# Query and key biases folded into the projection weights, and the feed-forward transposes moved to another accumulator bank with a new order of work

## The reference, cut to what matters

```
n  = (x - mean) * rsqrt(var + eps)            # over the 128 features
q  = (n * qn_w  + qn_b)  @ q_w + q_b          # 16 heads of 8
kv = (n * kvn_w + kvn_b) @ kv_w + kv_b        # k, v
q, k = rotary(q, x), rotary(k, x)             # cos/sin per token, scaled by a radius
q, k = layernorm over the 8 of a head
a  = softmax(q k^T / sqrt(8)) v @ out_w + out_b
x1 = x + a
z  = layernorm(x1); zp = z shifted one token back
r  = sigmoid((mu_r*z + (1-mu_r)*zp) @ W_r^T)
k2 = relu((mu_k*z + (1-mu_k)*zp) @ W_k^T) ** 2
x2 = x1 + r * (k2 @ W_v^T)
```

## Time and profile before

| | |
|---|---|
| runs, median | 1365.89 us |
| profiled execution | 1367.37 us, its span 1365.6 us |
| PE busy | 1284.8 us (94%) |
| DVE busy | 1122.7 us (82%) |
| ACT busy | 901.9 us (66%) |
| POOL busy | 504.9 us (37%) |
| steps of A with all stages (c = 6 to 31) | 26, mostly of 18.11 us |
| first and last row maximum (L790) | 35.5 and 605.1 us |

### The profile page before, as it was taken

How to read it: one execution, slowest core, us unless ns; L and a number is a source line. 1 busy time by engine, 2 the same in 40 slices (tenths; PEclk the granted TensorE clock), 3 DMA queues, 4 the chain that set the end, 5 groups by cost and what they waited for, 6 DMA issues and landing times.

```text
span 1365.6 us, 32982 instructions
## 1 busy us (share of the span) xinstructions
PE 1284.8 (94%) x10579; PEld 852.4 (62%) x10579; DVE 1122.7 (82%) x2849; ACT 901.9 (66%) x2504; POOL 504.9 (37%) x815
## 2 busy tenths in 40 slices
PE   7889999999999999888999999999999998999996
PEld 5445555555555555545566666666666665888885
DVE  5888999999999999876888888888888875778786
ACT  3278888888888888876565566556655653555563
POOL 5446666666666666533111111111111100232322
PEclk9999999999999999999999999999999999999998
DMA  2222332223333323210100010000000001232220
GB/s 80 77 76 81 82 79 76 73 78 80 82 91 103 99 69 84 67 51 17 32 28 29 28 49 28 30 28 28 27 30 25 20 17 41 79 87 82 85 86 27
DMA packets 101963, 79.61 MB, mean 58 GB/s; under 512 B 13780, under 2 KB 95124, under 8 KB 101796
## 3 DMA queue, kind: packets, MB, share of 16 engines
q1 hardware_dynamic: 100820, 76.99, 20.0%
q10 hardware_dynamic: 976, 0.54, 0.2%
HBM read 49.70 MB, written 27.79 MB: 57 GB/s over the span
## 4 chain that ended last, share of the span: by engine, by line
PE 49%; issue 1%; DVE 1%; ACT 1%; POOL 0%; POOLq 0%; DVEq 0%; ACTq 0%
PE b_psZ L1410 4%; PE b_psD L1331 4%; PE b_psZ L1342 4%; PE b_g L1394 4%; PE d_psO L1954 4%; PE b_g L1381 4%; PE d_psH L1946 4%; PE b_psM L1443 2%; PE b_psR L1387 2%; PE b_psL L1372 2%; PE b_psR L1403 2%; PE b_psD L1433 2%; PE b_psM L1455 1%; PE d_psG L1972 1%; PE d_psV L1985 1%
## 5 line engine op out<-in xcount | busy, mean ns | idle before, releaser
L790 DVE TENSOR_REDUCE a_MX<-a_psS 128x4 f32<-128x1024 f32 x248 | 303.2, 1223 | 44.6 <-PE a_psS L304 41.2
L591 ACT ACTIVATE a_PT<-a_psE 128x512 f32<-128x512 f32 x504 | 275.1, 604 | 59.3 <-PE a_psE L321 56.4
L1811 POOL TENSOR_TENSOR b_SWB<-b_b2col,b_SW 128x128 f32<-128x128 f32 x65 | 38.8, 597 | 346.2 <-ACT b_SW L1526 346.2
L335 PE MATMUL a_psV<-a_PT,a_VX 128*32 128x256 f32 x2048 | 137.0, 385 | 0.2 <-ACT a_PT L591 0.2
L1545 ACT ACTIVATE b_TH<-b_psZ 128x512 f32<-128x512 f32 x65 | 38.9, 598 | 128.7 <-PE b_psZ L1342 124.3
L304 PE MATMUL a_psS<-a_KS,a_QS 48*128 48x256 f16 x992 | 97.7, 275 | 22.1 <-DVE a_MX L790 20.6
L321 PE MATMUL a_psE<-a_QS,a_KS 50*128 50x256 bf16 x1008 | 97.5, 270 | 3.1 <-ACT a_PT L591 3.1
L1565 ACT ACTIVATE b_PR<-b_psL,b_mx 128x128 f32<-128x128 f32 x260 | 93.1, 369 | 0.9
L304 PEld LDWEIGHTS a_psS<-a_KS,a_QS 48*128 48x128 bf16 x992 | 29.1, 94 | 103.1 <-issue 48.2
L335 PEld LDWEIGHTS a_psV<-a_PT,a_VX 128*32 128x32 f32 x2048 | 53.4, 109 | 50.5 <-issue 27.5
L1693 DVE SCALAR_TENSOR_TENSOR b_HH<-b_TH,b_psZ 128x512 f32<-128x512 f32 x65 | 44.8, 689 | 44.1 <-ACT b_TH L1545 44.0
(11 more groups left out here) (298 smaller groups left out, 3426.4 us busy)
## 6 DMA issues: line engine op xcount, KB each, us to landing
a_KS<-kparts SPq DMA_DIRECT2D x63, 192.0 KB
a_QS<-qparts SPq DMA_DIRECT2D x126, 96.0 KB
qparts<-a_QP SPq DMA_DIRECT2D x64, 96.0 KB, 2.2
a_X<-x_in SPq DMA_DIRECT2D x32, 128.0 KB, 2.3
kparts<-a_KP SPq DMA_DIRECT2D x64, 64.0 KB, 2.1
x<-a_X SPq DMA_DIRECT2D x32, 128.0 KB, 1.8
b_X<-x SPq DMA_DIRECT2D x32, 128.0 KB, 2.2
zT<-b_XT SPq DMA_DIRECT2D x32, 128.0 KB, 1.7
```

The source lines that it names most:

```text
L335: mm = nc.tensor.matmul(psV[32 * h:32 * h + 32, 0:T], VX[:, b % UV, kt, at:at + 32], PT[:, gg, kt, h, :], start=(gg == 0 and kt == 0), sto ...
L591: nc.scalar.activation(PT[:, g % 2, :, h + s, :], shifted_bank(b, p, s), ACT.Exp).then_inc(S["exp"], 1)
L790: nc.vector.reduce_max(MX[:, b % 2, :].rearrange("q (s n) -> q s n", s=2)[:, :, 2 * p:2 * p + 2], score_banks(b, p)[:], AX.X).then_inc(S[" ...
```

## The change

The layer norm's output sums to zero over its 128 features, so the last feature is minus the sum of the others. The changed kernel leaves it out and puts a constant 1.0 in its place: `Z` gets only 127 normalised columns and a last column of ones, written once. The weights are rebuilt in the opening: each row minus the last row, times the gain, and as last row the bias. For this, PE has a new function `fold_weights` (five products of 128 columns and one of one column), DVE makes `gains`, and ACT copies the result to `wall`. Two constants are loaded more (`last`, 128x128, and `brow`, one row). With the biases in the weights, `cosine` and `sine` are one instruction of 512 columns each.

The second half moves work: `fz_t` writes bank psA for sequences before 26, ACT makes all four copies in slot 3, `ot` moves from slot 4 to 5; on PE, `on_t` and `z_t` move from slot 5 to slot 4, `ffn_kr` is split, with its k product placed between the scores and the shifted scores of slot 5 and its r products after, and `out_proj` goes before `hr_t`; on DVE, `x1` goes before `normed`.

```diff
-        nc.scalar.activation(wall[:, 0:P], wraw[:, 0:P], ACT.Copy, scale=vecs[:, 0:1]).then_inc(S["wall"], 1)
...
+        def weights():
+            act.wait_ge(S["param_ps"], 2)
+            nc.scalar.activation(wall[:, 0:2 * P], psS[:, 0, 0, :], ACT.Copy).then_inc(S["wall"], 1)
...
+        def fold_weights():
+            pe.wait_ge(const_in, EARLY)
+            for j in range(2):
+                pe.wait_ge(S["coefs"], 2 * j + 3)
+                nc.tensor.matmul(psS[:, 0, 0, j * P:(j + 1) * P], brow[:, 2, :], brow[:, j, :], start=True, stop=False)
+                nc.tensor.matmul(psS[:, 0, 0, j * P:(j + 1) * P], gains[:, j, :], wraw[:, j * P:(j + 1) * P], start=False, stop=True).then_inc(S["param_ps"], 1)
+            pe.wait_ge(S["coefs"], 6)
+            nc.tensor.matmul(psS[:, 1, 0, 0:P], gains[:, 2, :], wraw[:, 2 * P:3 * P], start=True, stop=True)
+            nc.tensor.matmul(psS[:, 1, 0, P:P + 1], last[:], wraw[:, 3 * P:3 * P + 1], start=True, stop=True).then_inc(S["param_ps"], 1)
...
         def cosine(b):
-            for k in range(2):
-                nc.vector.scalar_tensor_tensor(out=YC[:, k * T:(k + 1) * T], in0=psA[:, k * T:(k + 1) * T], scalar=bcol[:, k:k + 1], in1=cosT[:],
-                                               op0=ALU.add, op1=ALU.mult).then_inc(S["cosed"], 1)
+            nc.vector.tensor_tensor(YC[:].rearrange("q (k t) -> q k t", k=2), psA[:].rearrange("q (k t) -> q k t", k=2),
+                                    cosT[:].unsqueeze(1).broadcast_to([P, 2, T]), ALU.mult).then_inc(S["cosed"], 1)
...
         def fz_t(b):
+            if b < B - 6:
+                wait(pe, "square", b + 6)
+                wait(pe, "centred", b + 6)
...
+                to = (psE[0][:, 0, :] if b == B - 2 else psC if b >= B - 6 else psA)[:, t * P:(t + 1) * P]
...
-        def ffn_kr(b):
+        def ffn_k(b):
             wait(pe, "square", b + 6)
             wait(pe, "centred", b + 6)
+            wait(pe, "fzT", b, per=4)
             wait(pe, "mixed", b, per=2, done=1)
             nc.tensor.matmul(psA[:, 0:T], wk_t[:], FX[:, 1, :], start=True, stop=True)
+
+        def ffn_r(b):
             wait(pe, "mixed", b, per=2)
```

More of the change, by code:

```diff
@@ L87, in phase_a @@
     wraw, wall = sb("wraw", [P, 3 * P + 1]), sb("wall", [P, 3 * P + 1])
+    last, gains, brow = sb("last", [P, P]), sb("gains", [P, 3, P]), sb("brow", [1, 3, P])
     cosT, sinT = sb("cosT", [P, T]), sb("sinT", [P, T])
-    vecs, bcol = sb("vecs", [P, 8]), sb("bcol", [P, 3])
+    vecs, bcol = sb("vecs", [P, 8]), sb("bcol", [P, 1])
     ow, ow0, vbP = sb("ow", [P, P]), sb("ow0", [P, P]), sb("vbP", [P, P])
@@ L283, in bias_columns @@
             pe.wait_ge(const_in, EARLY)
-            for j, col in ((0, 1), (1, 3), (2, 3)):
-                mm = nc.tensor.matmul(psA[:, j:j + 1], wraw[:, j * P:(j + 1) * P], vecs[:, col:col + 1], start=True, stop=True)
-            mm.then_inc(S["bias_ps"], 1)
+            nc.tensor.matmul(psA[:, 0:1], wraw[:, 2 * P:3 * P], vecs[:, 3:4], start=True, stop=True).then_inc(S["param_ps"], 1)
+        def fold_weights():
[7 more added lines that the diff above has]
+            nc.tensor.matmul(psS[:, 1, 0, P:P + 1], last[:], wraw[:, 3 * P:3 * P + 1], start=True, stop=True).then_inc(S["param_ps"], 1)
         def out_bias():
@@ L354, in z_t @@
             wait(pe, "z", b)
+            if b == 0:
+                pe.wait_ge(const_in, EARLY)
+                pe.wait_ge(S["prep"], 3)
             if b == 1:
@@ L391, in centre @@
         def centre(b):
-            wait(pe, "cosed", b, per=2)
-            wait(pe, "sined", b, per=2)
-            wait(pe, "sined", b, per=2)
+            wait(pe, "cosed", b)
+            wait(pe, "sined", b)
             nc.tensor.matmul(psA[:], centre_w[:, 0, :], YC[:], start=True, stop=False)
@@ L479, in body @@
                     keep_busy({2: 1, 3: 1}.get(c, 0), psV[:, 0:T])
+                if p == 5:
+                    if on(c - 6):
+                        ffn_k(c - 6)
                 if on(c - 4):
@@ L514, in body @@
                         pv(c - 4, 2)
+                    if on(c - 5):
+                        out_proj(c - 5)
                     if on(c):
                         hr_t(c)
-                    if on(c - 5):
-                        out_proj(c - 5)
                 if p == 7:
@@ L526, in opening @@
         def opening():
+            z_t(0)
+            fold_weights()
             bias_columns()
-            z_t(0)
             proj_q(0)
@@ L663, in fz_t @@
             wait(act, "mixed", b - 1, per=2)
-            nc.scalar.activation(FC[:, part, :], psC[:, 0:T], ACT.Copy, scale=vecs[:, 4 + part:5 + part]).then_inc(S["fzT"], 1)
-            nc.scalar.activation(FP[:, part, 1:T], psC[:, 0:T - 1], ACT.Copy, scale=past[:, part:part + 1]).then_inc(S["fzT"], 1)
+            src = psA if b < B - 6 else psC
+            nc.scalar.activation(FC[:, part, :], src[:, 0:T], ACT.Copy, scale=vecs[:, 4 + part:5 + part]).then_inc(S["fzT"], 1)
+            nc.scalar.activation(FP[:, part, 1:T], src[:, 0:T - 1], ACT.Copy, scale=past[:, part:part + 1]).then_inc(S["fzT"], 1)
         def ffn_kr(b):
@@ L727, in scalar @@
         z_t(0)
+        weights()
         proj_v(0)
@@ L827, in sine @@
             wait(dve, "c_ps", b - 1)
-            for k in range(2):
-                nc.vector.scalar_tensor_tensor(out=YS[:, k * T:(k + 1) * T], in0=psA[:, k * T:(k + 1) * T], scalar=bcol[:, k:k + 1], in1=sinT[:],
-                                               op0=ALU.add, op1=ALU.mult).then_inc(S["sined"], 1)
+            nc.vector.tensor_tensor(YS[:].rearrange("q (k t) -> q k t", k=2), psA[:].rearrange("q (k t) -> q k t", k=2),
+                                    sinT[:].unsqueeze(1).broadcast_to([P, 2, T]), ALU.mult).then_inc(S["sined"], 1)
         def variance(b):
```

63 lines of the change are left out of this document (34 added, 29 removed).

## The result

The changed kernel took 1374.89 us (median of four runs, 1373.21 to 1375.22), the one before 1365.95 on the same chip (1365.3 to 1366.46): ratio **1.0056**, 95% interval 1.004 to 1.0072. It is slower: by 8.9 us between the medians, and by 7.2 between the spans of the two profiled executions, of which the one before was 1.4 above its median. The forecast was 1365.1 with a range of 1359 to 1371.5: wrong, in its likeliest case and in its range. The profiled execution took 1374.64, its span is 1372.8.

A forecast was written before the change was run, and what follows sets the result against it. PE, DVE and ACT were nearly full (17.10, 16.52, 15.43 of 18.11 us a step), none the whole bound. Opening +1.9, early steps -1.1 and full steps -1.6 gave 1365.1 us against the 1365.9 median; range 1359 to 1371.5.

The forecast's parts named there:

- Part 1: Slots 0 and 1 of full steps: cosine and sine as one instruction let centre start earlier, gaining 0.23 us a step.
- Part 2: Slots 3 to 7 of full steps: the new order costs 0.17 us a step, leaving -0.06 with the fold.
- Scores(5): PE, slot 4: on_t and z_t ahead of them take 0.46, so they start at 241.84 instead of 241.65, cost 0.19.
- The exponentials of slot 4: ACT: behind four copies taking 1.46 they start at 241.40 and end at 242.49, before at 241.76.
- The k product fills this time: PE, slot 5: it runs 242.07 to 242.67 while shifted(5) waits for ACT until 242.61; a tie, cover complete.
- `out_proj` and `hr_t`: Slot 6: with out_proj first, hr_t and then normed and the maximum come later, cost 0.13 to 0.23, taken as 0.17.
- the whole gain of slot 5: PE's possible gain of 0.35 at pv, claimed to be handed back entirely by ACT's delayed exponentials.
- The chain through `ffn_v`: Late exps(6), relu and POOL's square put ffn_v at about 247.6, the maximum 249.25 against 249.27: a tie, hidden.
- Slower: the k product holds shifted(5): Rival, PE slot 5: one gap of 0.2 passes through undiminished, step +0.14, 1370.3 us; chance 0.20.
- version with two gaps: Same rival with two PE gaps: +0.34 a full step and 1375 us, within that rival's chance of 0.20.
- Part 3: Early steps: steps 2 to 4 gain the full 0.36 each, -1.1 us; step 5 and steps 32 and 33 get 0.
- Part 4: Opening: four more PE products ahead of proj_q(0), at 0.48 each, cost +1.9 us, bounds +0.7 and +2.6.

The follow-up runs named there:

- fold_only: The changed kernel with the bias fold kept, but bank and order of slots 3 to 7 as before the change; 1362.45 us, ratio 0.9962.
- k_behind: The changed kernel with the k product of slot 5 moved behind the shifted scores on PE; 1363.98 us, ratio 0.9973.
- both_back: The changed kernel with the k product behind the shifted scores, hr_t ahead of out_proj and normed ahead of x1; 1360.03 us, ratio 0.9944.
- fb_open_warm: fb_open plus four dummy PE products ahead of hr_t in each of steps 2 and 3; 1357.18 us, ratio 0.9925.
- before_warm: The kernel before the change plus four dummy PE products ahead of hr_t in each of steps 2 and 3; 1365.17 us, ratio 0.9979.
- best: both_back with the shorter opening of fb_open and the dummy products of fb_open_warm in steps 2 and 3; 1354.95 us, ratio 0.9908.
- order_only: The changed kernel with the bias fold taken back, keeping only the new order of slots 3 to 7 and the bank; 1379.9 us, ratio 1.0095.
- hr_first: The changed kernel with hr_t ahead of out_proj on PE and normed ahead of x1 on DVE, as before; 1370.84 us, ratio 1.003.
- fb_open: fold_bank with one bias product instead of two, the bias column first and in psB, and proj_q(0) not waiting for bcol; 1357.67 us, ratio 0.9933.
- fold_bank: The changed kernel with all calls in the order before the change, but feed-forward transposes still in bank psA; 1361.4 us, ratio 0.9953.

## Why the prediction was wrong

**Part 1, the fold in the full steps: right.** "Gain 0.19 by the idle time, 0.25 by the starts; I take 0.23": slots 0 and 1 gained 0.23 after the change, and `fold_only` gained 0.23 a step. The instruction of 512 columns takes 0.69 and the next follows by 0.61, as its neighbour L864 said. The Trainium skill's rule ("Perfetto Trace Analysis", section "Tensor Engine Instruction (MATMUL, LD_WEIGHTS)"), that starts are the firm numbers, agrees: `centre` starts 0.26 earlier in its step (2.76 for 3.02) where the starts had promised 0.25 and the idle time 0.19, and 0.23 of it arrive at the maximum of slot 2.

**Part 2, the order: its mechanism was found, its outcome chosen wrongly.** Forecast +0.17 a step, measured +0.41. By its steps:

- Scores(5) were forecast at 241.84 and came at 241.97 in before's time (245.45 less 3.48): the two transposes take 0.59 to the next start (244.86 to 245.45), not 0.46.
- The exponentials of slot 4 were forecast to end at 242.49 and ended at 242.48 (244.86 + 1.10 less 3.48). The delay by the four copies was right to 0.01.
- "The k product fills this time: it starts 0.23 after scores(5), at 242.07 ... Tie; its cover is complete." **This is the step that failed.** It started 0.33 after them, at 242.30, and the shifted scores 0.63 after it, at 242.93 and not at 242.61. Against the 242.67 of the forecast, the terms are 0.13 for late scores, 0.10 for the k product's start, and 0.03 for 0.63 instead of 0.60. All three have one source, the distances taken: 0.23 is the distance of two narrow groups (scores, shifted scores) and 0.46 that of full ones, but here the kinds alternate. The 0.32 that part 1 took for a full group behind a narrow one was the right figure, and stood in the same text. On the other side the exponentials let shifted(5) go 0.05 after their end in `k_behind` (244.41 + 1.10 to 245.56), not 0.12. The hold was thus 0.40 (246.41 against 246.01), and taking it away gave 0.39.
- `out_proj` and `hr_t`: "taken as 0.17", measured 0.14.
- What is left without both is -0.12 (17.75 against 17.88 of `fold_only`): the forecast had the whole gain of slot 5 handed back, and two thirds are. -0.12 + 0.39 + 0.14 = 0.41. Part of it is a slip in the sum: 0.42 after 242.61 is 243.03, not 243.06. Another is the 0.05 for 0.12 above. With the k product behind them, the shifted scores of slot 6 show no idle time for ACT (`k_behind`: k product 245.89, r products 246.42, scores 246.96, shifted scores 247.19), so there PE's own order is as long as ACT's.
- The chain through `ffn_v` was called a tie, "hidden just so". It stayed hidden, in `both_back` too, where it had the least room.

The rival "Slower: the k product holds shifted(5)" (chance 0.20, 1370.3, "decides from shifted(5) at 242.74 on") named place, queue and outcome. Its price was half of what was measured: it reckoned with one gap of 0.2, for the k product as a wait that PE meets at the wrong time. Its version with two gaps came to 1375, but that is luck: it had +0.34 in a full step where +0.18 was measured, and the opening and the early steps made up the rest. It is no wait: 0.31 is also where a group of this kind starts when it waits for nothing (centre, 237.15 to 237.46), so the product itself, put between scores and shifted scores, was the cost. A margin of -0.06 was called a tie, and so free, on three distances of PE that were all too short, by 0.03 to 0.13. The Trainium skill's rule that PE may pull only weight loads ahead ("TensorE: Matmul & The Clock Gate", same section as in the prediction) spoke for this rival, which then got 0.20. The trace agrees: the shifted scores, free from 245.96 on, start behind the k product.

**Part 3, early steps: right where the clock stays up, and hidden by it here.** Forecast -1.1, measured -0.45 in steps 2 to 4 and +0.25 in step 5. `fb_open_warm` against `before_warm`, both at a granted clock of 1.00 throughout, shows the gain undisturbed: 15.04, 15.76, 16.64 against 15.38, 16.11, 17.01, together -1.06 (`best` is much alike in steps 3 and 4, but took 15.92 in step 2). In the changed kernel slot 0 of step 2 did gain 0.30, but slots 6 (2.59 for 2.24) of step 2 and 0 (3.68 for 2.99) of step 3 gave it back at the low clock, and the end of step 3 and the start of step 4 gained at the full one. After the change, on PE:

```profile
51.07 1.11 PE L423 MATMUL a_psB<-a_ident,a_HX 128*128 128x128 f32 x4 [2.01 <-ACT a_HX L665]
...
52.66 1.22 PE L351 MATMUL a_psV<-a_cosT,a_ident 128*128 128x256 f32 x2
```

and its windows:

```profile
50.00:54.00 4.00, 2.93 (x12) 2.01 (x13) 3.62 (x7) 1.65 (x4) 0.56 (x1) 0.58 0.00 0
```

The idle time of 2.01 is the one of before; the stretch at the low clock behind it is longer (0.58 in this window and 0.57 in the next; before 0.85 and 0.72 in the two shown above), while the second gap has none behind it. The column was in the trace of before, and the prediction did not read it. Step 5 lost 0.25, where 0 was forecast, by the order in slot 4 (2.13 for 1.81) and in slot 6 (2.81 for 2.64). Steps 32 and 33 lost 0.24 each, by slot 6: 2.61 for 2.19, and 2.18 again in `k_behind`, the same cause as in the full steps.

**Part 4, the opening: right in kind, too low.** Forecast +1.9, measured +3.0 (bounds 0.7 and 2.6, so outside; +2.7 to +4.0 in the five other traces with this opening). `proj_q(0)` came 2.61 later. "Three products of one column took 1.44, 0.48 each": the four added were counted at that price, but the first three of the new ones have 0.72 to 0.73 from start to start (7.80, 8.52, 9.25, 9.97). The constants came 0.26 later (7.21 for 6.95). The rest is the wait for `bcol`, which now comes at the end of the chain, and the 0.47 behind `proj_q(0)`, which no experiment has taken apart.

**The sum.** Forecast +1.9 - 1.1 - 1.6 = -0.8; measured +3.0 - 0.2 + 4.2 + 0.5 = +7.5. Of the miss of 8.3 us, 5.8 (70%) are the full steps. That these "repeat to 0.02" holds for 19 of the 26 before (18.11 or 18.12); seven lie between 18.03 and 18.47, and the table counts them all.

## What to carry to other kernels

An instruction that is moved ahead of another on an in-order engine delays it by all of its start-to-start distance that no other wait covers; a cover that is short by a few hundredths in the sum is no cover, and the order with the critical work first and the filler behind it is to be tried first. A change of several edits is worth taking apart even when it loses: here one edit gave 0.23 a step, another took 0.41, and the sum hid both. The granted clock of the early steps is to be read before tenths are counted there.

## What the runs showed of the hardware

- PE needs about 0.1 us more from one start to the next where full-array float32 groups (128*128 in the rows) and the narrow 16-bit ones of the scores (48*128, 50*128) alternate. The same k product has 0.44 to the next start between two full groups, in the kernel before:

```profile
242.87 0.38 PE L363 MATMUL a_psC<-a_ident,a_Z 128*128 128x128 f32 x2
243.09 0.60 PE L462 MATMUL a_psA<-a_FX,a_wk_t 128*128 128x256 f32 x2
243.53 0.61 PE L465 MATMUL a_psA<-a_wr_t,a_FX 128*128 128x128 f32 x4
```

  It has 0.53 behind a narrow group (245.89 to 246.42 in `k_behind`), and 0.63 between two narrow ones (after, `order_only`, `hr_first`). `z_t` has 0.22 to a full group here and 0.31 to the scores after (245.14 to 245.45). Why, no run settled.
- In the opening a float32 product with one row of weights takes as long as one with 128 rows: 0.79 and 0.80 for 128 columns. Where the two kinds alternate they are 0.72 to 0.73 apart; two products of 128 rows behind each other are 0.51 apart (9.33 to 10.35 for both, four instructions, in `fb_open`). How they are lined up costs more there than how many rows they hold.
- A DVE instruction that reads only SBUF (`hn` twice, 128x64, written to PSUM) took 0.23 on average in the traces where POOL's sums do not fall on it (0.23 in `before`, `fold_only`, `fold_bank`, `fb_open`, `before_warm`) and 0.64 to 0.66 in those where they do (`after`, `order_only`, `k_behind`, `hr_first`, `both_back`, `best`). The one before it, which reads one operand from PSUM, kept its 0.21 during such a sum (244.99). Nothing was run to tell why.
